# Windowed attention and MLP on one Trainium2 core: the projection of v issued one step earlier

## The reference

```python
y = roll(layernorm(x, g1, b1), (-2, -2), axis=(1, 2))     # then cut in windows of 128 tokens
qkv = xw @ qkv_w + qkv_b                                  # 32 -> 96
attn = softmax(q * SCALE @ k.T + bias + mask)             # 128 x 128, per window and head
o = (attn @ v) @ proj_w + proj_b                          # windows put back, rolled back
x = x + o
z = layernorm(x, g2, b2)
return x + gelu(z @ fc1_w + fc1_b) @ fc2_w + fc2_b        # 32 -> 128 -> 32
```

## Time and profile before

| | |
|---|---|
| median of 3 runs | 235.82 us (235.43 to 235.96) |
| the profiled execution's own time | 234.58 us |
| its span, first to last instruction | 232.8 us |
| mean granted TensorE clock | 0.994 of full speed |
| TensorE matmuls busy | 206.1 us (89%) |
| VectorE busy | 166.0 us (71%) |
| ScalarE busy | 146.1 us (63%) |
| GpSimd busy | 126.8 us (54%) |

### The profile page before, as it was taken

One profiled execution on the slowest core, in us unless ns is written; L12 is line 12 of the kernel. 1 busy time (PEld: TensorE's weight loads), 2 busy tenths in 40 slices (PEclk: granted clock), 3 DMA queues, 4 the chain that ended last, 5 costly groups with the idle time before them and its releaser, 6 DMA issues.

```text
span 232.8 us, 7983 instructions
## 1 busy us (share of the span) xinstructions
PE 206.1 (89%) x3280; PEld 114.8 (49%) x3280; DVE 166.0 (71%) x252; ACT 146.1 (63%) x213; POOL 126.8 (54%) x107
## 2 busy tenths in 40 slices
PE   0187489899999999999999999999999999979981
PEld 0144133466566556555665665556556556443210
DVE  5857565666777778768787878686776757857855
ACT  7453245765867586666766775756555655577881
POOL 6645990462339783896579477534552091150830
PEclk9999999999999999999999999999999999999997
DMA  6817645555503640463155125404440000000323
GB/s 205 238 55 249 202 149 159 189 161 161 174 22 124 195 146 9 162 205 103 49 165 158 55 96 179 130 26 138 136 143 5 6 1 4 4 3 0 135 102 128
DMA packets 25496, 26.59 MB, mean 114 GB/s; under 512 B 3744, under 2 KB 22944, under 8 KB 25344
## 3 DMA queue, kind: packets, MB, share of 16 engines
q1 hardware_dynamic: 24356, 25.10, 33.6%
q10 hardware_dynamic: 1104, 0.99, 1.5%
HBM read 17.03 MB, written 8.78 MB: 111 GB/s over the span
## 4 chain that ended last, share of the span: by engine, by line
issue 43%; POOL 39%; PE 6%; ACT 6%; DVE 3%; ACTq 1%; POOLq 1%; DVEq 0%
POOL rstd L351 16%; POOL X L374 4%; POOL parts L368 4%; POOL yn L361 4%; POOL xc L343 3%; POOL X L379 3%; PE ps L898 2%; ACT q_rows L692 1%; POOL mean L331 1%; ACT k_rows L692 1%; POOL var L337 1%; PE pq L898 1%; ACTq L48 1%; PE pch L786 1%; ACT k_rows L697 1%
## 5 line engine op out<-in xcount | busy, mean ns | idle before, releaser
L491 DVE TENSOR_REDUCE negm<-ps 128x8 f32<-128x1024 f32 x64 | 78.3, 1224 | 32.1 <-PE ps L834 31.6
L687 ACT ACTIVATE prob<-ps 128x1024 f32<-128x1024 f32 x64 | 65.5, 1023 | 39.9 <-PE ps L861 39.8
L351 POOL TENSOR_TENSOR rstd<-var,neghalf 128x16 f32<-128x16 f32 x16 | 47.5, 2967 | 17.1 <-DVE var L460 16.0
L848 PE MATMUL ps<-rel_j,id_b 96*32 96x512 bf16 x512 | 40.1, 387 | 2.2 <-ACT prob L687 2.2
L881 PE MATMUL pav<-prob,va 128*32 128x128 f32 x1024 | 41.1, 279 | 0.0
L881 PEld LDWEIGHTS pav<-prob,va 128*32 128x32 f32 x1024 | 24.1, 109 | 12.5 <-issue 5.0
L368 POOL TENSOR_TENSOR parts<-rest,parts 128x512 bf16<-128x512 f32 x16 | 18.4, 1157 | 20.5 <-ACT parts L671 20.5
L834 PE MATMUL ps<-k_rows,q_rows 64*128 64x128 bf16 x512 | 25.9, 223 | 2.8 <-DMA k_rows<-slots 2.8
L816 PE MATMUL ps<-rel_i,ident_b 64*64 64x512 bf16 x256 | 27.4, 418 | 0.2 <-DVE negm L491 0.2
L861 PE MATMUL ps<-q_rows,k_rows 64*128 64x128 bf16 x512 | 25.6, 220 | 0.0
L861 PEld LDWEIGHTS ps<-q_rows,k_rows 64*128 64x128 bf16 x512 | 14.5, 95 | 15.0 <-issue 14.9
(11 more groups left out here) (102 smaller groups left out, 318.0 us busy)
## 6 DMA issues: line engine op xcount, KB each, us to landing
slots<-parts SPq DMA_DIRECT2D x24, 256.0 KB, 2.4
q_rows<-slots SPq DMA_DIRECT2D x42, 128.0 KB
k_rows<-slots SPq DMA_DIRECT2D x42, 128.0 KB
X<-x_tok SPq DMA_DIRECT2D x8, 256.0 KB, 3.4
y_tok<-res SPq DMA_DIRECT2D x7, 256.0 KB, 2.0
q_rows<-slots SPq DMA_DIRECT2D x12, 64.0 KB, 2.3
k_rows<-slots ACTq DMA_DIRECT2D x12, 64.0 KB, 2.4
q_rows<-m_hi SPq DMA_DIRECT2D x32, 4.0 KB
```

The costliest lines, as they stand in the source:

```text
L351: pool.tensor_tensor(rstd[:, i, :], var[:, i, :], neghalf[:], ALU.pow).then_inc(rstd_done[i], 1)
L491: dve.tensor_reduce(dst, first_home(j)[:].rearrange("p (a u n) -> p a u n", u=2, n=TOK), AX.X, ALU.max, negate=True).then_inc(max_done, 1)
L687: act.activation(prob[:, j % NPROB, :], ps2[:], ACT.Exp).then_inc(exp_done, 1)
L848: pe.matmul(ps2[32 * c:32 * (c + 1), 512 * e:512 * (e + 1)], id3_b[0:96, :], rel_j[0:96, c, e].unsqueeze(2).to_broadcast([96, 2, 2, TOK]), ...
```

## The change

In TensorE's loop, project_v(b + 1) and the wait ahead of it are issued in step 4 instead of step 5. In step 4 it stands behind project_out and ahead of the weighted values. ScalarE's copy of the result stays in step 5. Nothing else is changed. (The condition p >= 0 changes nothing by itself: for p = -4, b + 1 is 0.)

```diff
--- before.py
+++ after.py
@@ -970,7 +970,7 @@
                         project_qk(n, (Q0, Q1))
                 if p % 4 == 2 and 0 <= (p - 6) // 4 < OCTETS:
                     tokens_first((p - 6) // 4)
-                if s == 5 and 1 <= b + 1 < B:
+                if p >= 0 and s == 4 and 1 <= b + 1 < B:
                     if n < B:
                         pe.wait_ge(rest_done, 2 * n + 2)
                     project_v(b + 1)
```

## The result

The changed kernel takes 237.28 us (median of 6 runs, 237.00 to 237.56) against 235.82 (6 runs, 235.43 to 235.96): ratio 1.0071, 95% interval 1.0057 to 1.0086, so 0.7% slower. (Both kernels have six runs here, where the text ahead speaks of three. So the two profiles lie 2.98 us apart and the medians 1.46.

The account below looks back on a forecast made before the run. TensorE's program order bounds the loop, each step at least the 2.4 us scores-exponential-bias loop; 6 x (0.87 - 0.58) - 0.13 = +1.6 us on 235.82 gives 237.4 us, range 236.6 to 238.9.

Parts of the forecast that it names:

- The hole in step 5: Step 5, images 1 to 6: without project_v, a 0.51 us wait for the exponential opens; -0.58 us of the 1.09.
- project_v behind project_out: Step 4, images 1 to 6: no hole to fill, so the eight added matmuls cost +0.87 us each image.
- The other bound: Step 4: project_v costs the 1.09 us it takes alone; as a rival +2.9 us, 238.7 us, chance 9%.
- Image 0: Steps 4 and 5 of image 0: the hole only changes its step; 5.61 us instead of 5.74, -0.13 us.
- The sum: Whole kernel: 6 x (0.87 - 0.58) - 0.13 = +1.6 us, median 237.4 us, 0.7% slower.
- ScalarE, and the wait for the remainder: ScalarE's step 5 has 0.3 us to spare, project_v's wait for the second remainder 0.9 us; both cost nothing.
- TensorE has room: Rival, steps 4 and 5: eight matmuls add in step 4 only what they free in step 5; 235.8 us, 6%.
- SP's queue falls behind: Rival, SP's sends of maxima: up to 0.58 us late, opening about 0.5 us holes in six images; near 240.4 us, 5%.
- Its sign, line 861 waiting for m_mid: TensorE's line 861 waiting for a DMA of m_hi or m_mid, named as showing the prediction wrong.
- the 3.3 us: SP's send of the maximum of step 0: time from its issue's end until wanted, called SP's tightest; nothing added.

Follow-up runs that it names:

- spare5: The changed kernel with one quarter of project_v computed a second time in step 5; 237.35 us, ratio 1.0067 to the kernel before.
- spare5x2: The changed kernel with two quarters of project_v computed a second time in step 5; 238.67 us, ratio 1.0118 to the kernel before.
- behind_max: The changed kernel with step 4's project_v issued behind the transposed maxima, not ahead of the weighted values; 237.44 us, ratio 1.0070 to the kernel before.
- again: The changed kernel run once more without any edit; 237.19 us, ratio 1.0077 to the kernel before.
- img0: The changed kernel with only image 0's project_v in step 4, the others back in step 5; 235.33 us, ratio 0.9985 to the kernel before.
- spare4: The changed kernel with one quarter of project_v computed a second time in step 4; 239.14 us, ratio 1.0137 to the kernel before.
- half45: The kernel before with half of project_v moved to step 4, half left in step 5, all seven images; 235.58 us, ratio 0.9999.
- img1to6: The changed kernel with project_v of images 1 to 6 in step 4, image 0's in step 5; 237.51 us, ratio 1.0098 to the kernel before.
- half57: Kernel before, project_v halved over steps 5 and 7, ScalarE's copy in step 7: 234.86 us; repeated: 234.62; image 0's halves in steps 4 and 5, copy in 5: 234.19.

## Why the prediction was right, point by point

The forecast was 237.4 us; 237.28 was measured. An agreement of 0.1 us is partly luck: the interval of the ratio is +1.3 to +2.0 us. For the profiled execution the working gave 236.2, and it took 237.56; the difference is the 0.42 us at the head, the late m_mid (0.69), image 0 (0.15) and 6 x 0.02 in the steps.

- *The hole in step 5* was the step that decides, and it held: -0.59 us instead of -0.58, with line 848 0.50 us later than it could be. spare5 and spare5x2 measure its size from inside.
- *project_v behind project_out*: 0.87 us by four transposes in the same place, 0.90 measured (3.65 - 2.75). The other bound, 1.09, was not approached. Reading a cost from a row with the same neighbour in the queue was worth 6 x 0.19 = 1.1 us of forecast. behind_max shows that another fp32 group ahead does as well.
- *Image 0*: -0.13 us forecast. again shows -0.14 for steps 4 and 5, img0 -0.34 +- 0.47 in the runs. In the changed kernel's own profile the two steps took 1.18 us more, which made up for a head start and was no cost of the move. SP's timeline there, and then before:

```profile
43.71 0.53 SPq L248 DMA_DIRECT2D q_rows<-m_hi  x1
44.30 0.52 SPq L248 DMA_DIRECT2D q_rows<-m_mid  x1
44.92 0.56 SPq L237 DMA_DIRECT2D k_rows<-slots  x1
```

```profile
43.28 0.53 SPq L248 DMA_DIRECT2D q_rows<-m_hi  x1
43.86 0.52 SPq L248 DMA_DIRECT2D q_rows<-m_mid  x1
44.48 0.57 SPq L237 DMA_DIRECT2D k_rows<-slots  x1
```

  SP's rows are 0.43 us later than before, as they already were near 31 us, before the change can act. But TensorE came to step 4 at 44.15 after, 44.88 before. It stood waiting for sends that were not earlier. Up to step 4 of image 0 the loop can't go faster than SP's sends and gathers land. I had not seen this. In this profile it also took away the 0.13 us that image 0 was to give: image 1 starts 0.45 us later than before, and 0.43 of it is SP's.
- *The sum*: 6 x 0.31 - 0.14 = +1.7 us by the rows of again, +1.5 in its runs.
- *ScalarE, and the wait for the remainder*: no cost, as said. The copy into va waits for nothing, project_v starts right behind project_out (0.55 us from start to start; the transposes in the earlier trace rows 0.54).
- *TensorE has room* fell. The Trainium skill (Perfetto Trace Analysis, "Identifying the Most-Contended Engine") judges headroom by weight-load busy time and achieved FLOPs; weight loads were busy 49% here. For TensorE's in-order list this said nothing: spare4 and spare5 show room of 0.5 us in the holes, and none for two more matmuls in step 4.
- *SP's queue falls behind* had 5% and is the one that I sized badly. Its sign, line 861 waiting for m_mid, came in the changed kernel's profile in two places, though I had written that I would be wrong then; again, with the same loss and no such wait, shows that the forecast didn't hang on it. In the steady loop it came in one image. Step 2 of image 3 (2.70 us before) took 3.39 us in the changed kernel, 3.43 in half45, 3.05 in spare5x2, 2.90 in img1to6; in image 4 it took 2.82 in spare4, 2.80 in behind_max, 2.76 in spare5. It was 2.70 in again, and in before, img0 and the three half57 kernels, which have 2.75 us in step 4. What lies behind it is in SP's timeline of the changed kernel:

```profile
100.64 2.66 SPq L237 DMA_DIRECT2D k_rows<-slots  x2
103.40 1.19 SPq L237 DMA_DIRECT2D q_rows<-slots  x2
104.68 1.19 SPq L237 DMA_DIRECT2D k_rows<-slots  x2
105.92 0.53 SPq L248 DMA_DIRECT2D q_rows<-m_hi  x1
106.49 0.54 SPq L248 DMA_DIRECT2D q_rows<-m_mid  x1
```

  Two gathers took 2.66 us to issue, the other pairs here 1.19. The issue of m_mid's send ended at 107.03, and TensorE would have been at line 861 at 108.89 (109.52 less its 0.63 of idle time): 1.9 us in between, where the earlier trace rows had 3.3. The data let it go on 2.5 us after the issue's end. But the 3.3 us, which I had called the tightest, was read from one image and is not: in image 4 of the same profile of before, the issue ended at 127.21 and line 861 started at 129.70, 2.5 us later and without a wait. A slow issue (two gathers 1.5 us over the usual here) is seen in other profiles too, again among them (0.9 us), without a wait. Nor does little time to spare make a wait by itself: in image 2 of img0 line 861 started 1.8 us after the issue's end, in image 1 of spare5 1.4 us, both without one. So in image 3 of the changed kernel the issue was slow and the landing was slow as well. That a longer step 4 leaves less to spare fits the list of kernels above, but no run shows it by itself. Why an issue or a landing is slow at times, and why behind_max, whose send isn't put off, still has 0.1 us of lateness in image 4, stays open.

## What to carry to other kernels

In an engine that looks full, look at each turn of the loop for the chain that goes out to another engine and back (here scores, exponential, bias: a floor of 2.4 us). Independent work placed between two turns is free up to the chain's wait and costs its full time above it, so moving work out of a turn that needs it into one that has enough gives back only the part above the wait (0.59 of 1.09 us here) and pays in full where it goes (0.90). The gain lies in spreading such work so that every turn just covers its wait; and the cost of an instruction group is best read from a row with the same kind of neighbour, since the ends of a group (0.2 us here) were paid once where fp32 groups of 128 rows stood together (behind project_out, behind the transposed maxima).

## What the runs showed of the hardware that I had not expected

TensorE's pace at the head of the loop differs from execution to execution of nearly the same program. Step 1 of image 0, which is mostly the q and k projection (line 786), took 3.66 us before, 2.50 in the changed kernel and 4.33 in again. Its line 786 in the changed kernel and in before:

```profile
36.63 1.13 PE L786 MATMUL pq<-yT,wqk_s 64*128 64x512 f32 x4 [0.28 <-DVE m_mid L497]
```

```profile
36.21 2.08 PE L786 MATMUL pq<-yT,wqk_s 64*128 64x512 f32 x4
```

Four such matmuls take 1.13 us in the changed kernel and 2.08 in the two others. The window from 36.5 to 38.5 us, in before and then in again (length, the engines' busy us and records, then the granted clock, DMA share, GB/s):

```profile
36.50:38.50 2.00, 2.00 (x8) 0.35 (x10) 0.79 (x1) 0.81 (x2) 0.00 (x0) 1.00 0.31 102
```

```profile
36.50:38.50 2.00, 2.00 (x8) 0.49 (x12) 1.04 (x1) 0.91 (x1) 0.00 (x0) 0.50 0.34 114
```

In again the granted clock is 0.50, which is 1.2 GHz, and from 40.5 on 0.99; in the changed kernel it is 1.00 (2.4 GHz) from 36.5 on. In before it also reads 1.00 from 36.5 to 38.5, though the matmuls took as long as at 1.2 GHz in again, so the record of the clock and its effect don't always agree. Much of the difference is given back before image 1: against SP's send of m_hi near 43.5 us, image 1 starts 12.44 us later in before, 12.46 in the changed kernel and 12.97 in again, so of the 1.83 us between the changed kernel and again 0.5 is left. How much of the spread of the runs this makes isn't shown.
